# Linear attention and a Mamba block in one kernel: q's normaliser moved to GpSimd ahead of the KV product, v transposed by the projection, and new places in the written-out order

## The reference

```
x = x + L0(gn(x))
x = x + L1(gn(x))
```

```
q, k, v, o = qkvo projection of x          # 4 x 128 channels
lepe = depthwise 5x5 convolution of v
q, k = elu(q)+1, elu(k)+1
eff  = softmax(SCALE * mean(q) . k)        # over the 256 positions
k    = k * eff * N
z    = 1 / (q . mean(k) + 1e-6)
kv   = rope(k)^T v / N                     # 16 x 16 per head
res  = (rope(q) kv) * z
out  = proj((res + lepe) * o)
```

```
h_t = exp(d_t * A) * h_{t-1} + (d_t * u_t) B_t
y_t = sum_s h_t C_t + u_t * D
y   = y * silu(z);  y = W_out y + skip_scale * xn
out = proj(layernorm(y))
```

## Time and profile before

| | us |
|---|---|
| median of 3 runs | 376.57 (375.87 to 378.69) |
| the profiled execution, its own time | 374.03 |
| its span in the profile | 372.2 |
| VectorE busy | 275.2 |
| TensorE busy | 274.4 |
| ScalarE busy | 220.1 |
| GpSimd busy | 201.5 |

### The profile page before, as it was taken

One profiled execution on the slowest core, in us unless ns is written; L12 is line 12 of the kernel. 1 busy time (PEld: TensorE's weight loads), 2 busy tenths in 40 slices (PEclk: granted clock), 3 DMA queues, 4 the chain that ended last, 5 costly groups with the idle time before them and its releaser, 6 DMA issues.

```text
span 372.2 us, 5571 instructions
## 1 busy us (share of the span) xinstructions
PE 274.4 (74%) x1882; PEld 128.2 (34%) x1882; DVE 275.2 (74%) x342; ACT 220.1 (59%) x408; POOL 201.5 (54%) x135
## 2 busy tenths in 40 slices
PE   2498796797678795977697759776987666964763
PEld 1264343353224242633363335333532212321321
DVE  1622228879410998699968996899699998999992
ACT  2413886566634795669656974698468737552211
POOL 0020201645290389358935893579458876876750
PEclk9999999589958899899989998999899875868598
DMA  7230407832248709960897079706960694196000
GB/s 261 83 87 3 112 15 279 307 77 56 77 129 277 308 30 247 299 234 25 211 314 253 26 211 307 260 23 175 336 268 8 223 295 169 42 344 236 0 14 14
DMA packets 27075, 61.73 MB, mean 166 GB/s; under 512 B 2992, under 2 KB 14896, under 8 KB 27056
## 3 DMA queue, kind: packets, MB, share of 16 engines
q1 hardware_dynamic: 26768, 60.88, 50.8%
q10 hardware_dynamic: 288, 0.61, 0.5%
HBM read 54.62 MB, written 6.86 MB: 165 GB/s over the span
## 4 chain that ended last, share of the span: by engine, by line
PE 26%; DVE 17%; issue 17%; DMA 12%; ACT 12%; POOL 10%; SPq 4%; POOLq 1%; DVEq 0%; ACTq 0%
POOL hst L958 6%; DVE hst L1199 4%; DMA V<-v_scratch 4%; PE F L430 4%; PE Y L583 3%; DVE DB L1174 3%; DVE hst L1186 2%; PE DB L556 2%; DMA Cs<-bc_scratch 2%; DVE DB L1170 2%; SPq L229 2%; PE F L378 2%; PE F L408 2%; DMA CCs<-cc 1%; POOL delta L931 1%
## 5 line engine op out<-in xcount | busy, mean ns | idle before, releaser
L958 POOL TENSOR_TENSOR hst<-hst,Cs 128x1024 f32<-128x1024 f32 x48 | 113.2, 2360 | 80.9 <-DVE hst L1199 80.6
L1199 DVE TENSOR_TENSOR_SCAN hst<-dec,DB 128x1024 f32<-128x1024 f32 x48 | 109.5, 2282 | 1.1
L843 ACT ACTIVATE dec<-dlt,negA 128x1020 f32<-128x1020 f32 x60 | 68.1, 1141 | 13.6 <-DVE hst L1189 9.3
L1174 DVE TENSOR_TENSOR DB<-DB,Bs 128x1024 f32<-128x1024 f32 x48 | 58.9, 1228 | 3.8 <-PE DB L556 1.5
L583 PE MATMUL Y<-hst,CCs 128*32 128x256 f32 x512 | 50.1, 429 | 11.7 <-POOL hst L955 9.5
L430 PE MATMUL F<-V,wpatch 128*32 128x256 f32 x512 | 38.2, 423 | 12.6 <-DMA V<-v_scratch 10.6
L955 POOL TENSOR_TENSOR hst<-hst,Cs 128x512 f32<-128x512 f32 x31 | 38.7, 1269 | 15.9 <-DVE hst L1186 15.9
L583 PEld LDWEIGHTS Y<-hst,CCs 128*32 128x32 f32 x512 | 14.8, 116 | 47.8 <-issue 31.4
L430 PEld LDWEIGHTS F<-V,wpatch 128*32 128x32 f32 x512 | 14.9, 115 | 29.7 <-DMA V<-v_scratch 12.2
L556 PE MATMUL DB<-du,CCs 32*128 32x512 f32 x64 | 21.2, 742 | 4.4 <-DVE DB L1170 3.3
L922 POOL TENSOR_TENSOR u<-u,oS 128x256 f32<-128x256 f32 x8 | 5.8, 724 | 31.3 <-DVE u L1094 31.3
(11 more groups left out here) (176 smaller groups left out, 509.7 us busy)
## 6 DMA issues: line engine op xcount, KB each, us to landing
Bs<-bc_scratch SPq DMA_DIRECT2D x32, 512.0 KB, 5.8
Cs<-bc_scratch SPq DMA_DIRECT2D x32, 512.0 KB, 6.5
dlt<-delta_scratch SPq DMA_DIRECT2D x15, 512.0 KB, 5.8
V<-v_scratch SPq DMA_DIRECT2D x32, 200.0 KB, 4.2
XN<-xn_scratch SPq DMA_DIRECT2D x28, 128.0 KB, 3.1
delta_scratch<-delta SPq DMA_DIRECT2D x16, 128.0 KB, 4.1
v_scratch<-vpad SPq DMA_DIRECT2D x8, 211.5 KB, 2.3
bc_scratch<-bc SPq DMA_DIRECT2D x8, 128.0 KB
```

The source lines that it names most:

```text
L843: af(dec[g % 4][:, :, 1:T], dlt[2 * j + g // SG][:, :, 1:T], ACT.Exp, scale=negA[:, g:g + 1]).then_inc(S("decay_ready"), 1)
L958: tt(hst[g % 4][:], hst[g % 4][:], Cs[g % SG][:], ALU.mult).then_inc(S("hc_ready"), 1)
L1174: v.tensor_tensor(flat(BIN), flat(DU), Bs[g % SG][:], ALU.mult).then_inc(S("b_ready"), 1)
L1199: v.tensor_tensor_scan(hst[g % 4][:], flat(dec[g % 4][:]), flat(BIN), 0.0, ALU.mult, ALU.add).then_inc(S("h_ready"), 1)
```

## The change

It does four things.

1. zS is no longer applied to the result: a new GpSimd product QZ = QR * zS comes at the end of front (segment 31), and TensorE multiplies KVM with QZ into the first half of F1, onto the convolution that lies there (start=False). So u1 and u2 on VectorE and u3 on GpSimd go; one VectorE instruction makes u3 = (F1 + blepe) * oS.
2. vS on ScalarE and the two transpositions on TensorE go. In their place TensorE makes v transposed as xg0^T times the weights of v, plus a product of a row of ones with the bias of v, for each of two blocks. xg0 must now live until kvT is done, so its next writing waits for kvT_done.
3. The skip term xk moves from ScalarE to GpSimd (tail, segment 27; for batch 0 in lead).
4. Nearly all segment numbers and all places are new. W0 grows by a row of ones and the bias row. QR and zS have one buffer instead of two, QZ has two.

The diff, cut to the edits of code and to some of the numbers (a comment names the engine and chain of what follows); the other numbers that the text speaks of stand below it:

```diff
         # SyncE front: vpad out, V4 in; tail: bc, spill
-                yield 6
+                yield 5
                 sp.wait_ge(S("vpad_ready"), b + 1)
                 sp.dma_start(v_dram, vpad[:]).then_inc(S("v_out"), 16)
-                yield 17
+                yield 11
                 sp.wait_ge(S("v_out"), 16 * (b + 1))
...
             def tail(b, j):
-                yield 17
+                yield 7
                 sp.wait_ge(S("bc_ready"), b + 1)
...
-                yield 17
+                yield 10
                 spill(b, j)
                 yield 18
                 load_delta(b, j, 0)
...
         # TensorE front
-                yield 22
+                yield 23
                 pe.wait_ge(S("lz_ready"), b + 1)
                 pe.wait_ge(S("qr_ready"), b + 1)
                 pe.wait_ge(S("tk_ready"), b + 1)
...
-                    last = nc.tensor.transpose(F0[:, 2 * P + P * blk:3 * P + P * blk], vS[:, P * blk:P * blk + P],
-                                               wt("ident"))
+                    mm(F0[:, 2 * P + P * blk:3 * P + P * blk], xg0[:, P * blk:P * blk + P], wt("wqkvo", 2 * C, C),
+                       start=True, stop=False)
+                    last = mm(F0[:, 2 * P + P * blk:3 * P + P * blk], wt("ones", rows=1), wt("bvrow", rows=1),
+                              start=False, stop=True)
                 last.then_inc(S("kvT_done"), 1)
-                yield 23
+                yield 28
                 pe.wait_ge(S("kvT_ready"), b + 1)
...
             def lepe(b, j):
-                    yield (20, 20, 23, 24, 28, 31, 31, 31)[n]
+                    yield (21, 22, 24, 26, 27, 27, 27, 31)[n]
-                                  start=(n == 0), stop=(n == ROUNDS - 1))
+                                  start=(n == 0), stop=False)
...
             def mid(b, j):
-                yield 4
+                yield 3
                 pe.wait_ge(S("kvm_ready"), b + 1)
-                pe.wait_ge(S("qr_ready"), b + 1)
-                mm(F1[:, T:2 * T], KVM[j][:], QR[j][:], start=True, stop=True).then_inc(S("res_done"), 1)
-                yield 7
-                pe.wait_ge(S("gms_ready"), 2)
-                pe.wait_ge(S("u2_ready"), b + 1)
-                mm(F1[:, T:2 * T], wt("ident"), X[:, bass.ds(b, 1), :].rearrange("p b t -> p (b t)"), start=True,
-                   stop=False)
+                pe.wait_ge(S("qz_ready"), b + 1)
+                mm(F1[:, 0:T], KVM[j][:], QZ[j][:], start=False, stop=True).then_inc(S("res_done"), 1)
+                yield 6
                 pe.wait_ge(S("u3_ready"), b + 1)
-                mm(F1[:, T:2 * T], wt("wproj"), u3[:], start=False, stop=True).then_inc(S("proj_done"), 1)
+                mm(F1[:, T:2 * T], wt("wproj"), u3[:], start=True, stop=False)
+                mm(F1[:, T:2 * T], wt("ident"), X[:, bass.ds(b, 1), :].rearrange("p b t -> p (b t)"), start=False,
+                   stop=True).then_inc(S("proj_done"), 1)
...
         # TensorE tail: xp, (z at 5), dt
-                yield 2
+                yield 5
                 pe.wait_ge(S("xn_shifted"), 16 * DCONV * b)
...
-                yield 6
+                yield 5
                 pe.wait_ge(S("zs_ready"), b + 1)
         # TensorE back: xk and y2, var2, projection
-                yield 16
+                yield 15
-                yield 22
+                yield 24
                 pe.wait_ge(S("sq2_ready"), b + 1)
-                yield 27
+                yield 30
                 pe.wait_ge(S("xl2_ready"), b + 1)
...
         # TensorE places, batch 1's front (qk, vo, eff, den, rope, kvT, kv), lead, batch 0's mid
-                    0: (67.073, 71.951, 100.7,),
+                    0: (73.75, 76.25, 96.25,),
-                    1: (42.683, 50, 54.878, 62.195, 64.634, 74.39, 79.268,),
+                    1: (38.75, 48.75, 53.75, 58.75, 63.75, 68.75, 78.75,),
...
         # ScalarE front
+                wait(act, "kvT_done", b)
                 af(xg0[:].unsqueeze(1), X[:, bass.ds(b, 1), :], ACT.Identity, bias=gms[:, bass.ds(b, 1), :],
...
-                yield 9
+                yield 8
                 act.wait_ge(S("vo_done"), b + 1)
...
-                yield 10
-                af(vS[:], F0[:, 0:T], ACT.Identity, bias=wt("bqkvo", 2, 1))
...
-                wait(act, "u1_ready", b - 1)
-                wait(act, "res_done", b - 1)
-                nc.scalar.copy(QR[j][:], F0[:, T:2 * T]).then_inc(S("qr_ready"), 1)
+                wait(act, "qz_ready", b)
+                nc.scalar.copy(QR[:], F0[:, T:2 * T]).then_inc(S("qr_ready"), 1)
...
         # ScalarE tail
-                yield 28
-                wait(act, "xc2_done", b - 1)
-                af(xk[j][:], XN[j][:, DCONV - 1:], ACT.Copy, scale=wt("skip")).then_inc(S("xk_ready"), 1)
...
         # ScalarE places: batch 0's mid (X, lnv, rs, xg, sq, lr, rr, XN), batch 1's front
-                    0: (43.056, 54.167, 59.722, 62.5, 68.056, 73.611, 76.389, 79.167,),
+                    0: (50, 55.714, 58.571, 64.286, 67.143, 75.714, 78.571, 84.286,),
-                    1: (37.5, 40.278, 45.833, 48.611, 51.389, 56.944, 65.278, 70.833, 81.944, 84.722, 90.278,),
+                    1: (32.857, 35.714, 38.571, 41.429, 47.143, 52.857, 61.429, 70, 72.857, 81.429,),
...
         # GpSimd
             def front(b, j):
-                yield 14
+                yield 15
...
-                yield 14
+                yield 20
                 tt(tk[:], QK[:, 1:2, :].broadcast_to([P, 2, T]), turns, ALU.mult).then_inc(S("tk_ready"), 1)
+                yield 31
+                pool.wait_ge(S("qr_ready"), b + 1)
+                pool.wait_ge(S("zS_ready"), b + 1)
+                wait(pool, "res_done", b - 1)
+                tt(QZ[j][:], QR[:], zS[:], ALU.mult).then_inc(S("qz_ready"), 1)
...
             def mid(b, j):
-                yield 8
-                pool.wait_ge(S("u2_ready"), b + 1)
-                pool.wait_ge(S("o_ready"), b + 1)
-                tt(u3[:], u2[:], oS[j][:], ALU.mult).then_inc(S("u3_ready"), 1)
+                yield from ()
...
+                yield 27
+                pool.wait_ge(S("xn_ready"), b + 1)
+                wait(pool, "xc2_done", b - 1)
+                tt(xk[j][:], XN[j][:, DCONV - 1:], wt("skip").broadcast_to([P, T]), ALU.mult).then_inc(S("xk_ready"), 1)
...
         # VectorE mid
-                yield 5
+                yield 8
                 dve.wait_ge(S("res_done"), b + 1)
-                dve.wait_ge(S("zS_ready"), b + 1)
-                v.tensor_tensor(u1[:], F1[:, T:2 * T], zS[j][:], ALU.mult).then_inc(S("u1_ready"), 1)
-                yield 6
-                dve.wait_ge(S("lepe_done"), b + 1)
-                dve.wait_ge(S("u1_ready"), b + 1)
-                v.scalar_tensor_tensor(out=u2[:], in0=F1[:, 0:T], scalar=wt("blepe"), in1=u1[:],
-                                       op0=ALU.add, op1=ALU.add).then_inc(S("u2_ready"), 1)
+                dve.wait_ge(S("o_ready"), b + 1)
+                v.scalar_tensor_tensor(out=u3[:], in0=F1[:, 0:T], scalar=wt("blepe"), in1=oS[j][:],
+                                       op0=ALU.add, op1=ALU.mult).then_inc(S("u3_ready"), 1)
...
         # VectorE places: batch 2's mid (after: u3, ga, nv, ms, xl), batch 3's front
-                    2: (126.333, 127.667, 133.444, 140.333, 147.222, 167.889,),
+                    2: (128.111, 129, 129.444, 129.667, 129.889,),
-                    3: (119, 127, 161, 174.778, 181.667, 188.556,),
+                    3: (126.5, 127.5, 128.333, 128.778, 129.222, 161,),
```

More of the change, by code:

```diff
@@ L78, in block_kernel @@
             ("qsum", 1), ("Mq", P), ("nmx", 1), ("sumE", 1), ("rE", 1), ("ksum", 1), ("Mk", P)))
-        vS, oS = sb("vS", [P, T]), [sb(f"oS_{j}", [P, T]) for j in range(2)]
+        oS = [sb(f"oS_{j}", [P, T]) for j in range(2)]
         vpad = sb("vpad", [P, WP * WP + SHIFTS[-1]])
@@ L291, in lead @@
                 load_bc(b, j, 0)
-                yield 26
+                yield 29
                 spill(b, j)
@@ L934, in tail @@
                 tt(du[j][:], delta[:], flat(xs[j][:]), ALU.mult).then_inc(S("du_ready"), 1)
+                yield 27
+                pool.wait_ge(S("xn_ready"), b + 1)
+                wait(pool, "xc2_done", b - 1)
+                tt(xk[j][:], XN[j][:, DCONV - 1:], wt("skip").broadcast_to([P, T]), ALU.mult).then_inc(S("xk_ready"), 1)
             def lead(b, j):
-                yield from ()
+                yield 14
+                pool.wait_ge(S("xn_ready"), b + 1)
+                wait(pool, "xc2_done", b - 1)
+                tt(xk[j][:], XN[j][:, DCONV - 1:], wt("skip").broadcast_to([P, T]), ALU.mult).then_inc(S("xk_ready"), 1)
             def back(b, j):
```

195 lines of the change are left out of this document (95 added, 100 removed), and 24 rows, old and new, of the table places.

## The result

| | before | after |
|---|---|---|
| median us (lowest to highest) | 376.22 (375.70 to 378.69) | 391.15 (390.38 to 395.48) |
| profiled execution: time, span | 374.03, 372.2 | 390.69, 388.7 |
| granted clock of TensorE | 0.892 | 0.887 |

A forecast was written before the change was run, and what follows sets the result against it. It took each loop period to be bound by a chain from scan 2 through delta, spill, V4, convolution and var2 to xl2. +3.0 - 1.0 - 0.4 + 0.3 = +1.9 on 374.03 gave 375.9, median 378.5, range 368 to 388.

The forecast's parts named there:

- VectorE's edits: VectorE per batch: u1 and u2 go, one PSUM operation comes, 0.4 us less; a loop period without waits 32.6 us.
- The head of a period: Loop period up to delta: Y's wait goes, lnu at about 11.3, delta ready at 17.1 us instead of 18.2.
- V4: Read-back of v's shifted copies, still behind the spill: same 8.9 us behind delta, V lands at 26.0 us, before 27.1.
- Behind V4: TensorE from V to xl2: collect 4 and kvT now ahead of var2, 7.1 us (6.1 to 7.8), before 3.3.
- The start: Prologue: XN of batch 0 comes 5.1 us later, so unit 0 begins 4.7 us later, at 65.2 (3.6 to 5.8).
- The hole: Stretch behind batch 0's units: KVM of batch 3 at 123.2, period 1 begins 3.0 us later (-1 to +9).
- the rival's side: Rival for the stretch before period 1: late V of batch 3, start 9 us later, median 384.5; chance 0.25.
- The last periods: Period 5 gains 0.4 us from VectorE's count, period 6 loses 0.3, period 7 and the end stay.
- kvT at full clock: Rival in the loop: V to xl2 6.1 us, each period 1.0 less, median 374.5; chance 0.09.
- VectorE becomes the bound: Rival in the loop: V4 4 us earlier, period 33.8 instead of 37.4, median 365; chance 0.25 with halfway cases.
- QZ holds tail back: Rival in the loop: GpSimd's QZ makes delta 2 us later, each period +1.9, median 386; chance 0.08.

The follow-up runs named there:

- e1: The change's new instructions in the order and places of the kernel before: 374.37 us, by the medians 1.002 of the kernel before.
- e9: The kernel after with 6 added unused products on TensorE ahead of its wait for V: 386.60 us, ratio 1.0369 to the kernel before.
- e3: The kernel after with SyncE asking for V4 ahead of bc's store and the spill of delta: 377.61 us, ratio 1.0113 to the kernel before.
- e4: The kernel after with var2 at segment 22 on TensorE instead of 24: 391.01 us, ratio 1.0459 to the kernel before.
- e6: The kernel after with TensorE's and ScalarE's work behind V back at the numbers of before: 395.04 us, by the medians 1.052 of the kernel before.
- e7: The kernel after with V4 of batch 3 ahead of bc's store of batch 1 in the prologue: 389.76 us, ratio 1.0375 to the kernel before.
- e10: The kernel after with V4 ahead of bc's store and the spill, and var2 at segment 22: 377.27 us, ratio 1.0128 to the kernel before.
- e11: e10 with all places of the prologue as before the change: 371.72 us, ratio 0.9902 to the kernel before.
- e12: The kernel before with V4 ahead of bc's store and the spill, and xp at segment 5 instead of 2: 367.85 us, ratio 0.9764 to it.
- e13: e11 with ScalarE's logarithm and exp of the second norm at segment 25 instead of 27: 370.41 us, ratio 0.9874 to the kernel before.
- e5: The kernel after with 24 added unused products on TensorE ahead of its wait for V: 448.07 us, ratio 1.1952 to the kernel before.

## Why the prediction was wrong

- **VectorE's edits**: right. A period less its waits (for lnu, for the product of L390, which VectorE did not wait for before, and for rr2) is 37.37 - 0.47 - 0.81 - 3.63 = 32.5 us in period 1 and 32.8 in period 3, forecast 32.6. Period 5 shows no gain, though (31.4 us, before 31.2; forecast -0.4).
- **The head of a period**: right within 0.2 in two periods. delta is ready at 17.3, 17.2, 17.9 and 17.5 (forecast 17.1), 1.5 us late over the loop; Y's wait went in two periods of four and is 0.5 us in another; cor waits 0.4 to 0.5 us for lnu, which comes at 12.6 and not at 11.3, where I had none.
- **V4: the first step that failed.** "With the same 8.9 us V lands at 26.0." It lands at 27.2, 27.5, 28.0 and 27.9: 6.5 us over the loop. Of these 5.0 are the distance, which is 9.9 to 10.4 us instead of 8.9, and 1.5 are delta. The four reads take SyncE 3.6 us to issue, before 3.2. The rows above show v's store, bc's and the spill within 2.1 us, before within 3.2; that these writes together slow V4 is argued, not tried alone. The distances point that way: with bc's store issued 0.6 us ahead of the spill (after) V comes 9.9 to 10.4 us behind delta, with 1.3 to 2.0 (before) 8.8 to 9.4, with 1.6 to 2.4 (e1) 7.7 to 8.4. The last two overlap, so it isn't the whole of it. I had read "V4 stands behind the spill in both" as "the distance stays".
- **Behind V4: the mechanism right, the clock's part of the term mis-sized.** The queue of collect 4 and kvT ahead of var2 is there. V to xl2 took 6.1 us in period 1, at the full clock, and 8.7, 10.4 and 7.7 in the others, two of them above my upper end of 7.8: over the loop 4.5 us more than four times 7.1. I had priced kvT alone at the half clock, from before, where that clock lasted some 3 us; in period 3 everything ran in it for 12 us. The rows of periods 1 and 3 give the four parts at either clock: two rounds 0.9 and 1.7 us, collect 4 with its D term 1.0 and 1.9 (I had 1.0), kvT 2.6 and 4.6 (I had 1.8 to 3.5), var2 to xl2 1.7 and 2.2. So kvT was too cheap at both clocks, and that 6.1 is also the lower end of my range is luck: my 3.3 for the rest had a half clock in it, and at the full one that rest is 2.6. e9 takes the half clock away and gets 6.1 everywhere. Another 1.1 us falls behind xl2 in period 3, 0.96 of it the wait for du's broadcast, late for the same reason: 6.5 + 4.5 + 1.1 = 12.1, the whole miss of the loop.
- **The start**: right, with some luck. Unit 0 at 65.3, forecast 65.2. The six profiles with this prologue and no added products (after, e3, e4, e6, e7, e10) have it between 62.4 and 68.0, since batch 1's first product (L378) begins anywhere from 30.0 to 35.5; from there it is 31.1 to 32.5 us to unit 0, in the kernel before 27.9 and in e1 28.1. So the places cost 3 to 4.6 us here.
- **The hole**: on the rival's side. I forecast the store of bc at 109.5 (110.05) and V at 116.1; V landed at 120.12, beyond the 119 from which that rival decided, and four rounds took 3.6 us at the half clock instead of 2.9. Period 1 began 6.9 us later, not 3.0. But e7 shows that little of this delay is worth anything by itself.
- **The last periods**: period 6 gained 1.9 us instead of losing 0.3. VectorE's timelines have waits of 0.37 us for Y, 1.24 for lnu and 0.89 for du there before, and 0.18, 0.69 and none after: 1.6 of the 1.9.
- **The rivals.** "kvT at full clock" expected the plain products that replace the transpositions to bring the clock back. With everything behind V in the old order and plain products, the half clock lasted some 3 us in periods 3 and 4 of e6 and 9 to 10 in periods 1 and 2, and 7 in period 2 of e1; before, with transpositions, some 3 in each period. No help from the plain products shows. "VectorE becomes the bound" was dismissed on the program order and that is where the gain lay: one number in that order (e3) was worth 3.5%. "QZ holds tail back" did not come.
- By the recorded ratios to the kernel before, with the quotients of the medians in brackets: after 1.047 (1.040). V's place is 3.5% (2.9%; e3), clear of noise, and the clock's part is within it, since TensorE no longer idles there. The clock behind V alone is 1.0% (0.3%; e9), not clear of noise, though its 8.2 us stand in the loop's trace. The prologue's places are 2.3% (1.5%) once the loop is mended (e10, e11). The instructions, 374.4 against 373.7 us (e1), nothing. The parts aren't a sum: e3 gains more than the loop had lost, and what is saved in one place partly returns in the next.

## What to carry to other kernels

Where an engine's order is fixed and one transfer arrives late, ask first what stands ahead of that transfer in its queue, and move it before moving what waits for it: moving one waiter (e4) only hands the wait to the next. Whatever then slips behind in the queue needs room of its own in the order (xp behind Y in e12, the logarithm ahead of the decay in e13). Price all of TensorE's work behind a wait of 2 to 3 us at both clocks, not only the instructions seen slow in one trace; six useless products in the gap took 8.2 us off the loop here (e9), though little of it was left at the end, and 24 of them cost 57 us (e5).
